# The place of one transposing copy and the split of six substitution rows in a gated delta rule kernel

## What is computed

```
q, k, v = causal_dwconv(x @ Wq.T), causal_dwconv(x @ Wk.T), causal_dwconv(x @ Wv.T)   # 4 taps
g, beta = log_sigmoid(x @ Wg.T), sigmoid(x @ Wb.T)
k = k / |k|,  q = q / 8
for each token:                                     # state S of each head is 64 x 64
    S = exp(g) * S + beta * (outer(v, k) - outer(S k, k))
    o = S q
x = layernorm(x + o @ Wo.T)
x = layernorm(x + experts(x) + shared(x))
```

## Time and profile before

| | us |
|---|---|
| runs of the kernel | 2053.08, 2043.18, 2047.87; median 2047.87 |
| profiled execution | 2054.14, span 2052.3 |
| TensorE busy (matmul) | 1729.6 (84% of the span) |
| VectorE busy | 1151.2 (56%) |
| GpSimd busy | 963.6 (47%) |
| ACT busy | 667.6 (33%) |
| granted TensorE clock, mean | 0.93 |

### The profile page before, as it was taken

How to read it: one execution, slowest core, us unless ns; L and a number is a source line. 1 busy time by engine, 2 the same in 40 slices (tenths; PEclk the granted TensorE clock), 3 DMA queues, 4 the chain that set the end, 5 groups by cost and what they waited for, 6 DMA issues and landing times. The chain is left out here.

```text
span 2052.3 us, 81073 instructions
## 1 busy us (share of the span) xinstructions
PE 1729.6 (84%) x35340; PEld 1329.0 (65%) x35340; DVE 1151.2 (56%) x2901; ACT 667.6 (33%) x1290; POOL 963.6 (47%) x1261
## 2 busy tenths in 40 slices
PE   6678999898899899998999999967699999398960
PEld 5246666666666666666666666666588888397850
DVE  1377667666676667666767676752255555122214
ACT  1334343433344334333343434411111211032323
POOL 0244434443434343433443444331277777577863
PEclk9799999999999999999999999987899999699985
DMA  6344443445444544444344534432555553199647
GB/s 246 93 96 89 117 113 90 104 100 118 101 95 97 123 104 92 93 113 113 87 107 106 116 87 101 114 59 49 180 157 157 165 170 117 49 275 249 116 73 246
DMA packets 530241, 250.10 MB, mean 122 GB/s; under 512 B 423504, under 2 KB 497872, under 8 KB 528992
## 3 DMA queue, kind: packets, MB, share of 16 engines
q1 hardware_dynamic: 511456, 225.93, 42.5%
q0 software_dynamic: 18432, 18.99, 5.3%
HBM read 173.49 MB, written 71.37 MB: 119 GB/s over the span
## 5 line engine op out<-in xcount | busy, mean ns | idle before, releaser
L382 PE MATMUL delta_p_j<-delta_xt,delta_w 128*128 128x512 f32 x768 | 416.4, 668 | 38.6 <-DMA delta_xt<-in_xt 18.0
L582 DVE SCALAR_TENSOR_TENSOR delta_kq<-delta_hist,cw,delta_kq 128x512 f32<-128x512 f32 x384 | 316.5, 824 | 37.4 <-ACT delta_kq L712 28.4
L705 ACT ACTIVATE delta_hist<-delta_p_j 128x512 f32<-128x512 f32 x192 | 114.4, 596 | 512.8 <-PE delta_p_j L382 512.8
L842 POOL TENSOR_TENSOR delta_sd<-state,eg_end 128x256 f32<-128x256 f32 x128 | 104.7, 818 | 349.8 <-DVE state L648 349.8
L382 PEld LDWEIGHTS delta_p_j<-delta_xt,delta_w 128*128 128x128 f32 x768 | 140.3, 203 | 165.0 <-issue 125.0
L1202 POOL DMA_INDIRECT slot_tokens<-mix_tokens,mix_slot x192 | 190.0, 990 | 65.5 <-issue 60.9
L444 PEld LDWEIGHTS delta_p_i<-delta_kkq,rt 64*64 64x64 f32 x4096 | 139.2, 141 | 120.1 <-DVE delta_kkq L632 88.7
L444 PE MATMUL delta_p_i<-delta_kkq,rt 64*64 64x32 f32 (+1 forms) x4096 | 149.0, 218 | 61.1 <-DVE delta_kkq L632 60.6
L622 DVE TENSOR_TENSOR delta_outer<-delta_xi,delta_kb 128x15 f32<-128x15 f32 (+7 forms) x480 | 117.7, 245 | 126.6 <-DMA delta_kb<-n_scratch 115.6
L632 DVE TENSOR_TENSOR delta_kkq<-delta_xd,delta_p_i 128x384 f32<-128x384 f32 (+2 forms) x192 | 78.1, 407 | 138.9 <-PE delta_p_i L444 137.6
L412 PE MATMUL delta_p_xy<-delta_w,delta_hist 64*64 64x64 f32 x6144 | 136.8, 220 | 2.6 <-issue 2.6
(11 more groups left out here) (144 smaller groups left out, 3575.2 us busy)
## 6 DMA issues: line engine op xcount, KB each, us to landing
delta_xd<-x_scratch SPq DMA_DIRECT2D x256, 128.0 KB
delta_w<-in_wqkv SPq DMA_DIRECT2D x64, 480.0 KB
w<-in_w SPq DMA_DIRECT2D x64, 352.0 KB
delta_eg<-eg_rows SPq DMA_DIRECT2D x128, 130.0 KB
n_scratch<-delta_kkq SPq DMA_DIRECT2D x128, 128.0 KB
mix_ot<-ot SPq DMA_DIRECT2D x16, 1024.0 KB
w<-in_w SPq DMA_DIRECT2D x64, 176.0 KB
ot<-delta_o SPq DMA_DIRECT2D x32, 256.0 KB
```

The lines of the kernel that those rows point to most:

```text
L382: mm = pe.matmul(p_j[:, :], w[e][:, (ch * 3 + n) * 128:(ch * 3 + n) * 128 + 128], xt[m // 8 % 2][:, ch * 512:ch * 512 + 512], start=ch == ...
L582: ve.scalar_tensor_tensor(out, view(hist[e], i * 2 * 518 + tap, (259, 2), (1, 256)), cw[:, column:column + 1], out, ALU.mult, ALU.add).the ...
L705: ac.activation(view(hist[e], n * 518 + 3, (259, 2), (1, 256)), p_j[:, :], ACT.Copy)
L842: po.tensor_tensor(view(sd, 0, (128, 2), (C, 2), (1, C)), view(state, first_pair(group) * 128, (C, 2), (128, 2), (1, C)), view(s.eg_end, g ...
```

## The change

Two statements move in the hand-written order; no instruction is added or removed, and the orders of TensorE, GpSimd and SyncE stay as they are.

```
@@ VectorE, odd slots
                 if odd:
-                    substitute(subst_group, range(0, 3))
+                    substitute(subst_group, range(0, 4))
                 if is_macro(before):
                     inverse_lengths(before)
                 if is_macro(mi):
                     horner(mi, rx_done, 16, y1_out)
                 if two_:
                     update(*two_)
                 if odd:
-                    substitute(subst_group, range(3, 6))
+                    substitute(subst_group, range(4, 6))
                 if is_macro(mi):
                     horner(mi, ry1_done, 32, y2_out)
@@ ACT
                 if is_macro(before):
                     keys_values(before)
-                if t % 2 == 0 and 0 <= (t - 4) // 2 < NG:
-                    turn_inverse((t - 4) // 2)
                 if is_macro(m):
                     history(m, 1, proj_v)
                 if two_:
                     solved(*two_)
                 if is_macro(m):
                     last_tap(m, 2, yv[m % 2][:, :], tap_v)
+                if t % 2 == 0 and 0 <= (t - 4) // 2 < NG:
+                    turn_inverse((t - 4) // 2)
                 if two_ and two_[1] == 3:
                     output(two_[0])
```

## The result

The changed kernel took 2090.92 us (median of 4, 2080.64 to 2093.59), the kernel before 2050.47 (median of 4, 2043.18 to 2069.21). The ratio is 1.0166, with a 95% interval of 1.0106 to 1.0227: slower by some 34 us.

What follows compares the result with a forecast made beforehand. A ring of VectorE's rows, the turned copy, SyncE and the load of `kb` was taken as the bound; 0 + 11.3 + 11 + 0 = 22 us on the median 2047.87 gave 2071, range 2058 to 2093.

Steps and rivals of the forecast that it cites:

- the ring: Pace-setting cycle over two macro tiles: VectorE 19.61 us from row 0 to last row, then SyncE and DMA 21.16 us.
- Rival 1: TensorE's freed wait for `u` does bound: about 40 us gained, less 11.3, 2018, or 2008 with no delay; chance 0.07.
- the lower clock: TensorE's clock falling around `ry1` in ten more loops: 0.34 us on VectorE plus 0.8 of delay each, 11 us.
- The late copy: Even slot: turned copy behind V's three ACT copies starts mostly 0.62 or 0.88 us late in 14 groups, 11.3 us.
- the second kind: Groups where ACT idles only 1.54 to 2.03 us before the turned copy, so moving it delays it; 14 of 30.
- Nothing on SyncE takes this up: Claim that the turned copy's delay passes on, since SyncE's wait for the store of `xit` ends last.
- the loop at 636.66: Loop with granted clock 0.57 over 642 to 646 us, from which 0.34 us on VectorE was taken.
- the loop at 842: Loop idle 2.69 us before `ry1`, last row 20.73 us after `kb`; as upper bound 2.2 us each, 62 us.
- rival 4: TensorE's clock falls in every loop: up to 62 us, 2093 to 2110; chance 0.12.
- The four rows: Fourth row ahead of the reciprocal: `ry1` 0.48 us later, GpSimd holds the next row instead, horner y2 unmoved; taken as 0.
- Rival 2: The row moved ahead of the reciprocal escapes GpSimd, saving 1.4 us a loop: 2017; chance 0.05.
- the term that I had named as a bound: GpSimd, 0.48 us later, may meet the even slot's first convolution differently: up to 0.3 us a loop either way, 9 us.

Runs made afterwards that it cites:

- e1: Only the turned copy moved, the six rows left three and three, against the kernel before: ratio 1.0141 (1.0104 to 1.0179).

## Why the prediction held, and which of its sizes were off

**The bound.** Right: the ring. Shortening it by SyncE's order alone gained 4.4%, and TensorE's waits for `u` could be taken away (e1) without gain. Rival 1 (the freed wait does bound) is refuted for this kernel; its sum, by the way, gives 2019 and not 2018. With the shorter ring the freed wait does pay: 40 us of waits for `u` and a gain of 32. That the rest went into late copies and rows would fit in size, but is not shown.

**The sum by loops.** From the timelines of the middle, per loop, before and after: row 0 to the last row's end 19.59 and 20.42 us; last row to the copy 0.04 and 0.64; copy to the next row 0 21.71 and 21.53. That is +0.83, +0.60 and -0.18, and 1.25 in all; times 26, 21.6 + 15.7 - 4.7 = 33 us. The 21.6 are two things, the rows (6) and the lower clock (16), as below.

**The late copy.** Forecast: 11.3 us for 14 groups of the second kind and 8 (0.8 each) for ten more. In the trace 19 of 26 copies are late, 15.7 us in all, most of them by 0.89; 17 of the 19 are in loops with one of the longer stretches of lower clock. "Nothing on SyncE takes this up" does not hold in general: with the copy twice, more lateness was mostly taken up by a quicker landing. For this pair the landing takes up under 1 us of the 15.7 (4.33 and 4.30 us a loop); the rest of the 4.7 lies in SyncE's stretch from the odd slot's `kkq` store (625.82 in the earlier trace rows) to the issue of `kb`, 7.24 and 6.89 us on the mean. What makes that stretch shorter stays open, so the late copies' net cost is 15.7 us at most, 11 if all of the 4.7 is set against it, and no time shows it.

**The lower clock.** The term that was mis-sized. I had 0.34 us on VectorE for each of ten more loops, 3.4 us, taken from the loop at 636.66. It is some 16 us: of the 0.83 us by which the mean loop grew on VectorE, 0.23 are the rows', and 0.60 times 26 are left. The number of loops with a fall, the step that I trusted least, grew by only four; it was the price of one that was wrong. The fall comes with the long idle stretch ahead of `ry1`, lasts over 8 us, and costs the loop some 1.5 us, as in the loop at 842 that stood as the upper bound. Half of the loops go that way (13 of 26), which is rival 4 in half of the loops; eight keep the full clock. With TensorE kept busy 2.4 us longer the whole loss goes away. So the mechanism is right, and the nearest row for its price would have been at 844.35, since the longer wait was certain and a copy of that loop was the likelier outcome.

**The four rows.** Right on VectorE and GpSimd: the fifth row's instructions are now the held ones (0.88 and 0.97 us), GpSimd's hold was only handed on, and horner y2 starts 4.86 us after row 0 as it did (4.88). By the rule of the Trainium skill ("SBUF — State Buffer", Who interferes with whom) named in the prediction, the trace agrees: the held row takes 0.88 and 0.97 us, where a row of nearly that width takes 0.22 undisturbed, while GpSimd's weightings take 1.04 each. Rival 2 is refuted. Wrong in the sum: I took 0 and it is 0.42%, some 9 us. Most of that is the term that I had named as a bound and left out of the sum, GpSimd meeting the even slot's first convolution 0.48 us later: 0.23 us in every undisturbed loop, 6 us over the 26. The rest goes with the clock: eight of its loops run long where three did. I had named the 0.48 us by which `ry1` comes later without carrying it to TensorE's idle stretch; that it is this delay that brings the longer falls there is likely, but not shown by a run of its own.

**What was expected of the profile.** The wait for `kb` rose to 159.7 us (130 or more), copies are late in over half the groups, and TensorE's wait before `ry1` rose from 0.78 to 2.93 us a loop (1 to 2.5 more), as said. So the sizes were off in opposite ways: the clock's part too small by some 12 us and the rows' by 6, the late copies' too large, 19 us for 15.7 at most. The sum of 22 us is two thirds of the measured 34. That the time still lies in the range is owed to the width of the range and in part to errors that offset each other, not to the sizes.

## What to carry to other kernels

A wait of the busiest engine is worth its length only if the next thing behind it does not wait for a ring through another queue; follow the freed time to the next wait before counting it. Where the engine is TensorE, joining two idle stretches into one longer one can cost more than the idle time saved, by the clock; if the stretch can't be shortened, a little work without use in it is worth trying, and its result has to be measured: in the kernel before, which had few long stretches, it gained nothing clear of noise. And a delay of an engine that is not on the path can have a price there: here 0.48 us on GpSimd made two VectorE instructions wait instead of one. Last, look at the queue that only issues transfers: a few statements in another order there gained 4.4%, more than twice what the change on the engines cost.

## What the runs showed of the hardware that I had not expected

One long idle stretch brought a longer fall of the clock than two short ones. In the loop of the earlier trace rows at 638.54, two waits of 1.15 and 1.44 us, the lower clock lasted some 4 us (0.57 over 642 to 646) and cost VectorE 0.34 us; behind one of 3.97 us (the loop at 820.98) it lasted over 8 us and cost 1.7 us against the 19.50 of an undisturbed loop. Whether the single stretch or the sum of idle time decides is not separated by these runs. Multiplying a constant for 2.4 us in each loop (1.7 us of idle time stayed in the one shown) kept the clock at 0.98 over the stage. The Trainium skill ("TensorE: Matmul & The Clock Gate", What's actually happening) says that the clock follows how busy the array was; the trace agrees in that and adds that by far not every such stretch is punished: the wait of 2.48 us at 390.90 was followed by full speed, and with the change eight of 26 loops kept the full clock, where I had read the page as a fall in nearly every loop.

Over 26 loops of two kernels, a store issued 0.65 us later landed 0.47 us sooner after its issue (4.19 and 3.72 us, up to the next issue of SyncE), so that a delay at a queue's entry need not come out at its end.
